# Moving eight LoRA matmuls and their copy ahead of a layer norm's broadcast matmul, in the feed-forward stage of a two-stage transformer layer

## The chip, the cores and the metric

One Trainium2 chip, all 8 of its cores. Each core gets 2 of the 16 sequences (2 x 2048 tokens, width 1024) and the same weights, and runs the same program without exchange with the others. The metric is the device time of one execution in microseconds (us), that of the slowest core.

## The reference

```python
x = x + attn(layernorm(x), ...)      # local window attention, latent attention, gates
x = x + ffn(layernorm(x), ...)

def _qlora_linear(x, q, scale, bias, la, lb):
    w = _dequant(q, scale)                       # 4-bit values, a scale for every 16 inputs
    base = einsum('btd,od->bto', x, w) + bias
    lora = einsum('btr,or->bto', einsum('btd,rd->btr', x, la), lb)   # rank 32
    return base + lora

h = x                                            # ffn
for blk in range(3):
    y = _qlora_linear(h, qweights[2*blk], ...)
    y = _layernorm(y, ln_gamma[blk], ln_beta[blk])
    y = gelu(y)
    y = _qlora_linear(y, qweights[2*blk+1], ...)
    h = y + h
```

## The kernel before

The program is written out instruction by instruction for each engine: PE (TensorE, matmuls), DVE (VectorE), ACT (ScalarE), POOL (GpSimd) and SP (which issues transposing DMAs). Each small function adds a stretch to one engine's list. What stands in a list runs in that order; between engines there are counting semaphores (`te` for PE, `ve`, `ev1` and `ev2` for DVE, `sc` for ACT), and a `wait_ge` holds back all that is written behind it on its engine. There is no scheduler: the order of the calls is the order of the work.

The first stage (up to some 2070 us) is the attention, over 16 tiles of 256 tokens. Then the six 1024 x 1024 weight matrices are dequantized into SBUF. The second stage, from about 2210 us, is the feed-forward part, again over 16 tiles of 256 tokens, in 8 pairs of a tile A and a tile B. A pair goes through the three blocks k = 0, 1, 2. Activations lie feature-major, as 8 chunks of 128 features x 256 tokens. For one tile and one block the pieces are:

- `b_Y1`: the first linear map. PE multiplies h by the LoRA factor (L1233, 8 matmuls into bank C6 of psC, 32 x 256); DVE copies the result to SBUF (L1244); PE computes 8 column groups, each of 8 matmuls L1261 and one L1267 that adds the LoRA part. Groups 0 to 3 go to four regions of psA. Group 4 needs region 0 again, group 5 region 1, and so on, and waits until DVE has evacuated groups 0 and 1 (`ev1`).
- `b_L1e`: DVE evacuates the 8 groups with the bias (L1283, two at a time as PE finishes them) and squares them (L1291).
- `b_L1m`: PE sums values and squares over the features with a vector of ones (L1305, L1311, 8 matmuls each).
- `b_L1b`: five one-row operations on DVE (L1326 to L1338, the last a reciprocal), a square root on ACT (L1346, before which it loads its table), and one matmul L1352 on PE that broadcasts mean and inverse deviation to 128 partitions.
- `b_L2`: DVE adds and multiplies them into the tile, two passes over 128 x 2048 (L1366, L1372).
- `b_Ga`: the gelu on ACT, 8 operations (L1386).
- `b_Y2`: the second linear map, built as the first (L1401, L1412, L1429, L1435), with six regions. `b_E2`: DVE evacuates it and adds h (L1456, for the last block L1464); the last count of `ev2` says that the new h is ready.

The two tiles are interleaved: while one is in its layer norm, the other's Y1 runs. The order in a pair, with the part on which the change bears:

```python
for k in range(3):
    b_L1m(A, k)
    b_L1b(A, k)
    if k > 0:
        b_Y1(Bst, k)
        b_L2(A, k)
        b_L1e(Bst, k)
    else:
        b_L2(A, k)
    b_Ga(A, k); b_Y2(A, k); b_E2(A, k)
    b_L1m(Bst, k)
    b_L1b(Bst, k)
    ...                       # the same with b_Y1(A, k + 1) for k < 2
```

"A round" below is the time from one broadcast matmul L1352 to the next; there are 48, and in 32 of them a Y1 follows the broadcast.

Of the kernel before, what the change touches and what calls it, by code (L numbers as in the profile page):

```python
# [68 lines left out]
def build_program():  # L69
# [30 lines left out]
    with contextlib.ExitStack() as es:  # L100
# [10 lines left out]
        ar_t = sb("arena", [128, AC], BF16)  # L111
# [14 lines left out]
        A = lambda n: ar.alloc("A", n)  # L126
# [112 lines left out]
        def I(sem, inst, k=1):  # L239
            sem.n += k  # L240
            inst.then_inc(sem.h, k)
            return sem.n
# [837 lines left out]
        def bank_wait(t, b):  # L1080
            if b in pbank:
                eng, val = pbank[b]
                t.wait_ge({'ve': ve.h, 'sc': sc.h, 'te': te.h,
                           'ev1': ev1.h, 'ev2': ev2.h}[eng], val)

        def bank_set(b, eng, val):
            pbank[b] = (eng, val)
# [123 lines left out]
        def b_hio(st, sbk):  # L1211
            a, bb = st['ha'], st['hb']
            hin = a if sbk != 1 else bb
            hout = bb if sbk != 1 else a
            return o_hF + hin * NCH * TILE, o_hF + hout * NCH * TILE

        def b_Y1(st, sbk):
            i0 = 2 * sbk
            hin_o, _ = b_hio(st, sbk)
            ti, pp = st['ti'], st['pp']  # L1220
            btr_o = st['btr']

            @block.tensor
            def _(t, i0=i0, hin_o=hin_o, sbk=sbk, ti=ti, pp=pp):
                if sbk == 0:
                    t.wait_ge(dtr[pp].h, h0_done_d[ti])
                    if ti == 0:
                        t.wait_ge(ve.h, deq_done)
                else:
                    t.wait_ge(ev2.h, st['h_ready'])  # L1230
                bank_wait(t, 'C6')
                for c in range(NCH):
                    mm = t.matmul(psC[0:32, 0:TILE],  # L1233
                                  laS[:, i0 * NCH * 32 + c * 32:i0 * NCH * 32 + (c + 1) * 32],
                                  V(hin_o + c * TILE, TILE),
                                  start=(c == 0), stop=(c == NCH - 1))
                I(te, mm)
            st['btr1_te'] = te.n

            @block.vector  # L1240
            def _(v, i0=i0, btr_o=btr_o):
                v.wait_ge(te.h, st['btr1_te'])
                bp = (i0 % 2) * 64
                v.tensor_scalar(ar_t.ap()[bp:bp + 32, btr_o:btr_o + TILE],  # L1244
                                psC[0:32, 0:TILE], 1.0, None, ALU.mult)
                bank_set('C6', 've', I(ve, v.drain()))
            st['btr1_ve'] = ve.n

            te_y1 = {}

            @block.tensor
            def _(t, i0=i0, hin_o=hin_o, btr_o=btr_o):
                ev0 = ev1.n
                for oc in range(NCH):
                    reg = Y1REGS[oc % 4]
                    if oc >= 4:
                        t.wait_ge(ev1.h, ev0 + ((oc - 4) | 1) + 1)
                    else:
                        bank_wait(t, Y1BANKS[oc % 4])
                    for c in range(NCH):  # L1260
                        t.matmul(reg, wTv(i0, c, oc * 128, 128),  # L1261
                                 V(hin_o + c * TILE, TILE),
                                 start=(c == 0), stop=False)
                    if oc == 0:
                        t.wait_ge(ve.h, st['btr1_ve'])
                    bp = (i0 % 2) * 64
                    mm = t.matmul(reg,  # L1267
                                  lbS[bp:bp + 32,
                                      (i0 // 2) * 1024 + oc * 128:(i0 // 2) * 1024 + oc * 128 + 128],
                                  ar_t.ap()[bp:bp + 32, btr_o:btr_o + TILE], start=False, stop=True)  # L1270
                    te_y1[oc] = I(te, mm)
            st['te_y1'] = te_y1

        def b_L1e(st, sbk):
            i0 = 2 * sbk
            te_y1 = st['te_y1']
            y1o, sqo = st['y1F'], st['sqF']

            @block.vector
            def _(v, i0=i0, y1o=y1o):  # L1280
                for oc in range(NCH):
                    v.wait_ge(te.h, te_y1[min(oc | 1, NCH - 1)])
                    v.tensor_scalar(V(y1o + oc * TILE, TILE),  # L1283
                                    Y1REGS[oc % 4],
                                    biasS[:, i0 * 8 + oc:i0 * 8 + oc + 1], None, ALU.add)
                    bank_set(Y1BANKS[oc % 4], 'ev1', I(ev1, v.drain()))  # L1286
            st['y1_evac'] = ev1.n

            @block.vector
            def _(v, y1o=y1o, sqo=sqo):  # L1290
                v.tensor_tensor(V(sqo, NCH * TILE), V(y1o, NCH * TILE),  # L1291
                                V(y1o, NCH * TILE), op=ALU.mult)
                I(ve, v.drain())
            st['sq_ve'] = ve.n
# [19 lines left out]
                I(te, mm)  # L1314
            st['sums_te'] = te.n

        def b_L1b(st, sbk):
            sro, bro = st['srow'], st['brow']
            sb_name, sb_ps, sb_off = st['stb']
            sr = lambda a, bn: ar_t.ap()[0:1, sro + 2 * a:sro + 2 * a + 2 * bn].bitcast(F32)  # L1320
            br = lambda a, bn: ar_t.ap()[0:1, bro + a:bro + a + bn]

            @block.vector
            def _(v, sb_ps=sb_ps, sb_off=sb_off):
                v.wait_ge(te.h, st['sums_te'])
                v.tensor_scalar(br(0, TILE), sb_ps[0:1, sb_off:sb_off + TILE],  # L1326
                                -1.0 / D, None, ALU.mult)
                v.drain()
                v.tensor_tensor(sr(0, TILE), br(0, TILE), br(0, TILE), op=ALU.mult)
                v.drain()  # L1330
                v.scalar_tensor_tensor(sr(TILE, TILE),
                                       sb_ps[0:1, sb_off + 256:sb_off + 256 + TILE],
                                       1.0 / D, sr(0, TILE),
                                       op0=ALU.mult, op1=ALU.subtract)
                v.drain()
                v.tensor_scalar(sr(TILE, TILE), sr(TILE, TILE), EPS, None, ALU.add)
                v.drain()
                v.reciprocal(sr(2 * TILE, TILE), sr(TILE, TILE))  # L1338
                I(ve, v.drain())  # L1339
            st['var_ve'] = ve.n  # L1340

            @block.scalar
            def _(s):
                s.wait_ge(ve.h, st['var_ve'])
                with nc.allow_low_precision(reason="bf16 LN inv for broadcast matmul"):
                    I(sc, s.activation(br(TILE, TILE), sr(2 * TILE, TILE), AF.Sqrt))  # L1346
            st['sig_sc'] = sc.n

            @block.tensor
            def _(t, sb_ps=sb_ps, sb_off=sb_off):  # L1350
                t.wait_ge(sc.h, st['sig_sc'])
                mm = t.matmul(sb_ps[:, sb_off:sb_off + 512], onesR[0:1, :], br(0, 512),  # L1352
                              start=True, stop=True)
                I(te, mm)
            st['bc_te'] = te.n
# [156 lines left out]
        for pair in range(nbt_total // 2):  # L1512
            A = b_state(2 * pair)
            Bst = b_state(2 * pair + 1)
            b_Y1(A, 0)
            b_L1e(A, 0)
            b_Y1(Bst, 0)
            b_L1e(Bst, 0)
            for k in range(3):
                b_L1m(A, k)  # L1520
                b_L1b(A, k)
                if k > 0:
                    b_Y1(Bst, k)
                    b_L2(A, k)
                    b_L1e(Bst, k)
                else:
                    b_L2(A, k)
                b_Ga(A, k)
                b_Y2(A, k)
                b_E2(A, k)  # L1530
                b_L1m(Bst, k)
                b_L1b(Bst, k)
                if k < 2:
                    b_Y1(A, k + 1)
                    b_L2(Bst, k)
                    b_L1e(A, k + 1)
                else:
                    b_L2(Bst, k)
                    b_tail(A)
                b_Ga(Bst, k)  # L1540
                b_Y2(Bst, k)
                b_E2(Bst, k)
            b_tail(Bst)
            for tj in (2 * pair + 2, 2 * pair + 3):
                if tj < nbt_total:
                    emit_x2load(tj)
                    emit_ln2_h0(tj)
# [87 lines left out]
```

## Time and profile before

| | us |
|---|---|
| median of 2 runs | 4145.25 |
| the two runs | 4129.68, 4160.83 |
| the profiled execution: device time | 4170.05 |
| its span, first to last instruction, core 4 (the slowest) | 4168.5 |
| the shortest span of a core (core 1) | 4114.9 |
| PE matmuls busy, share of the span | 2569.3, 62% |
| PE weight loads busy | 1621.0, 39% |
| DVE busy | 1981.8, 48% |
| ACT busy | 1009.4, 24% |
| POOL busy | 77.0, 2% |

The times are those of one profiled execution on its slowest core, so sums are made against its own 4170.05 us and not against the median. Matmuls overlap in the engine and their ends are modelled, so the sum of their durations is not the time that PE needs for them; distances from one start to the next are. "Granted clock" is the share of TensorE's full 2.4 GHz that the chip granted in a stretch. In the chain of work that ended last, PE has 44% of the span, DVE 26%, ACT 10%, and 9% is "issue": short pauses in which an engine waits for nothing that the profile shows.

### The profile page before, as it was taken

The numbers are of one execution on the slowest core, as the hardware profiler recorded it, in microseconds if no ns is written. First come the engines' busy times: TensorE is split into PE (matmuls) and PEld (weight loads), VectorE is DVE, ScalarE is ACT, GpSimd is POOL, SyncE is SP. The second block draws the span as 40 slices with busy tenths as digits, with TensorE's granted clock in tenths as the row PEclk, the third lists the DMA queues.
The fourth block names the chain that finished last, engine by engine and source line by source line (L and its number), as shares of the span: only waits on it lengthen the run. The fifth ranks groups of instructions, "written<-read, shape, count | busy, mean of one in ns | idle before, by whom it ended". The sixth has DMA issues, their size and how long they took to land.

```text
span 4168.5 us, 57513 instructions; the slowest of 8 cores (4114.9 to 4168.5 us)
## 1 busy us (share of the span) xinstructions
PE 2569.3 (62%) x20161; PEld 1621.0 (39%) x20176; DVE 1981.8 (48%) x3863; ACT 1009.4 (24%) x1729; POOL 77.0 (2%) x126
## 2 busy tenths in 40 slices
PE   0566666566667666666435757567576666757666
PEld 0344443344444434444203434344343433434333
DVE  1445544454545444555324544445454444545544
ACT  0122233322223333222372212212121221212121
POOL 1000000000000000000020000000000000000000
PEclk9766766666666556666557867778797888878787
DMA  9021111111111111111331010100102010010201
GB/s 136 13 34 29 29 26 29 29 34 29 29 31 24 29 34 29 29 29 26 45 105 36 1 51 1 41 11 6 46 1 51 1 36 16 6 46 1 51 1 31
DMA packets 259705, 128.18 MB, mean 31 GB/s; under 512 B 229232, under 2 KB 233504, under 8 KB 259424
## 3 DMA queue, kind: packets, MB, share of 16 engines
q1 hardware_dynamic: 228864, 79.72, 9.5%
q0 software_dynamic: 30560, 44.79, 5.8%
q8 instruction: 167, 2.74, 0.3%
q14 instruction: 114, 0.93, 0.1%
HBM read 61.99 MB, written 25.17 MB: 21 GB/s over the span
## 4 chain that ended last, share of the span: by engine, by line
PE 44%; DVE 26%; ACT 10%; issue 9%; DMA 5%; another core or an unknown queue 2%; DVEq 2%; SPq 1%; ACTq 1%; POOL 0%; POOLq 0%
PE psA L1261 7%; PE psB L1429 5%; PE psA L1429 4%; DMA arena<-arena 3%; ACT arena L794 3%; PE psA L772 3%; PE psB L891 3%; PE psA L384 2%; DVE arena L1372 2%; DVE arena L1366 2%; PE psA L413 2%; DVE arena L1338 2%; DVE arena L806 2%; DVE arena L1283 2%
## 5 line engine op out<-in xcount | busy, mean ns | idle before, releaser
L1261 PE MATMUL psA<-arena,wbig 128*128 128x256 bf16 x3072 | 457.4, 299 | 24.6 <-DVEq L1286 24.6
L772 PE MATMUL psA<-arena 64*128 64x256 bf16 x960 | 249.9, 391 | 170.1 <-ACT arena L794 170.1
L1261 PEld LDWEIGHTS psA<-arena,wbig 128*128 128x128 bf16 x3072 | 292.6, 105 | 137.8 <-issue 56.4
L806 DVE TENSOR_TENSOR arena<-arena,mlocS 128x512 bf16<-128x512 bf16 x480 | 204.1, 425 | 228.2 <-ACT arena L794 203.7
L1346 ACT ACT_TABLE_LOAD x48 | 61.6, 1283 | 1008.3 <-DVEq L1339 1008.3
L1283 DVE TENSOR_SCALAR arena<-psA,biasS 128x256 bf16<-128x256 f32 x384 | 185.9, 484 | 237.3 <-PE psA L1267 191.3
L794 ACT ACTIVATE arena<-psA 128x512 bf16<-128x512 f32 x480 | 260.9, 594 | 59.9 <-PE psA L772 58.8
L1429 PE MATMUL psA<-arena,wbig 128*128 128x256 bf16 x1536 | 222.6, 293 | 0.0
L384 PE MATMUL psA<-wbig,arena 128*128 128x512 bf16 x497 | 140.6, 448 | 131.9 <-DMA arena<-arena 121.8
L1429 PE MATMUL psB<-arena,wbig 128*128 128x256 bf16 x1536 | 205.5, 278 | 0.0
L772 PEld LDWEIGHTS psA<-arena 64*128 64x128 bf16 x960 | 72.9, 106 | 319.2 <-issue 310.2
L1386 ACT ACTIVATE arena<-arena,lnbS,lngS 128x256 bf16<-128x256 bf16 x384 | 193.9, 586 | 0.6
L545 ACT ACT_TABLE_LOAD x16 | 20.5, 1283 | 710.1 <-PE psC L475 710.1
L1233 PE MATMUL psC<-arena,laS 128*32 128x256 bf16 x384 | 84.1, 394 | 159.6 <-DMA arena<-arena 98.7
L833 PE MATMUL psB<-arena 128*128 128x64 bf16 x960 | 79.7, 209 | 150.4 <-DVEq L809 134.1
L1401 PE MATMUL psC<-arena,laS 128*32 128x256 bf16 x384 | 63.9, 322 | 167.2 <-ACT arena L1386 167.2
L1429 PEld LDWEIGHTS psA<-arena,wbig 128*128 128x128 bf16 x1536 | 143.5, 104 | 54.2 <-issue 16.2
L1429 PEld LDWEIGHTS psB<-arena,wbig 128*128 128x128 bf16 x1536 | 136.3, 99 | 38.5 <-issue 0.4
L1386 ACT ACT_TABLE_LOAD x48 | 61.6, 1283 | 345.8 <-DVEq L1375 345.8
L459 PE MATMUL psA<-arena,wbig 128*128 128x256 bf16 x1024 | 128.4, 293 | 24.9 <-DVEq L906 22.0
L833 PEld LDWEIGHTS psB<-arena 128*128 128x128 bf16 x960 | 73.3, 121 | 177.4 <-issue 177.4
L891 PE MATMUL psB<-arena,wbig 128*128 128x256 bf16 x1024 | 131.3, 295 | 12.2 <-DMA arena<-arena 9.1
(166 smaller groups left out, 4304.8 us busy)
## 6 DMA issues: line engine op xcount, KB each, us to landing
y<-arena SPq DMA_DIRECT2D x16, 1024.0 KB, 4.3
arena<-qT POOLq DMA_DIRECT2D x48, 256.0 KB, 2.6
arena<-x_in POOLq DMA_DIRECT2D x16, 512.0 KB, 6.9
x2scr<-arena SPq DMA_DIRECT2D x16, 512.0 KB, 3.4
arena<-x2scr POOLq DMA_DIRECT2D x16, 512.0 KB, 6.2
arena<-arena SPq DMA_TRANSPOSE x224, 3.2
wbig<-wq POOLq DMA_DIRECT2D x1, 2048.0 KB, 18.3
wbig<-wk POOLq DMA_DIRECT2D x1, 2048.0 KB, 30.4
```

The costliest lines, as they stand in the source:

```text
L384: mm = t.matmul(reg, V(o_XF + c * TILE + tc * 128, 128), wv_(o_wv + c * 1024 + og * 512, 512), start=(c == 0), stop=(c == NCH - 1))
L459: mm = t.matmul(reg, wv_(o_wk + c * 1024 + oc * 128, 128), V(o_XF + c * TILE, TILE), start=(c == 0), stop=(c == NCH - 1))
L772: mm = t.matmul(reg[:, hh * 256:(hh + 1) * 256], ar_t.ap()[0:64, o_KR + h * 2 * W + sl * W + koff: o_KR + h * 2 * W + sl * W + koff + 128] ...
L794: sc_exp[nb] = I(sc, s.activation(dst, reg, AF.Exp))
L806: v.tensor_tensor(dst.rearrange("p (g q) -> p g q", g=2), dst.rearrange("p (g q) -> p g q", g=2), mkv, op=ALU.mult)
L833: mmA = t.matmul(avreg[:, h * 64:(h + 1) * 64], st, V(o_VR + vsl * 1024 + h * 64, 64), start=first, stop=last)
L891: mm = t.matmul(reg, wv_(o_wo + c * 1024 + oc * 128, 128), V(o_mixF + c * TILE, TILE), start=(c == 0), stop=(c == NCH - 1))
L1233: mm = t.matmul(psC[0:32, 0:TILE], laS[:, i0 * NCH * 32 + c * 32:i0 * NCH * 32 + (c + 1) * 32], V(hin_o + c * TILE, TILE), start=(c == 0), ...
L1261: t.matmul(reg, wTv(i0, c, oc * 128, 128), V(hin_o + c * TILE, TILE), start=(c == 0), stop=False)
L1283: v.tensor_scalar(V(y1o + oc * TILE, TILE), Y1REGS[oc % 4], biasS[:, i0 * 8 + oc:i0 * 8 + oc + 1], None, ALU.add)
L1386: I(sc, s.activation(V(go + c * TILE, TILE), V(go + c * TILE, TILE), AF.Gelu, bias=lnbS[:, sbk * 8 + c:sbk * 8 + c + 1], scale=lngS[:, sbk ...
L1429: t.matmul(reg, wTv(i1, c, oc * 128, 128), V(go + c * TILE, TILE), start=(c == 0), stop=False)
```

## The change

`b_Y1` is split after the copy of the LoRA product (`b_Y1a` up to there, `b_Y1b` the column groups), and `b_L1b` is split before the broadcast matmul (`b_L1v` the row operations and the root, `b_L1c` the broadcast). In the pair's loop the other tile's `b_Y1a` now stands between `b_L1v` and `b_L1c`. At the start of a pair `b_Y1` is still called whole.

```diff
-        def b_Y1(st, sbk):
+        def b_Y1a(st, sbk):
...
             st['btr1_ve'] = ve.n
 
+        def b_Y1b(st, sbk):
+            i0 = 2 * sbk
+            hin_o, _ = b_hio(st, sbk)
+            btr_o = st['btr']
             te_y1 = {}
...
             st['te_y1'] = te_y1
 
+        def b_Y1(st, sbk):
+            b_Y1a(st, sbk)
+            b_Y1b(st, sbk)
+
...
-        def b_L1b(st, sbk):
+        def b_L1v(st, sbk):
...
             st['sig_sc'] = sc.n
+
+        def b_L1c(st, sbk):
+            bro = st['brow']
+            sb_name, sb_ps, sb_off = st['stb']
+            br = lambda a, bn: ar_t.ap()[0:1, bro + a:bro + a + bn]
 
             @block.tensor
...
             for k in range(3):
                 b_L1m(A, k)
-                b_L1b(A, k)
+                b_L1v(A, k)
                 if k > 0:
-                    b_Y1(Bst, k)
+                    b_Y1a(Bst, k)
+                b_L1c(A, k)
+                if k > 0:
+                    b_Y1b(Bst, k)
                     b_L2(A, k)
                     b_L1e(Bst, k)
                 else:
...
                 b_L1m(Bst, k)
-                b_L1b(Bst, k)
+                b_L1v(Bst, k)
                 if k < 2:
-                    b_Y1(A, k + 1)
+                    b_Y1a(A, k + 1)
+                b_L1c(Bst, k)
+                if k < 2:
+                    b_Y1b(A, k + 1)
                     b_L2(Bst, k)
                     b_L1e(A, k + 1)
```

PE's list in the second stage, where a tile B's layer norm (statistics in psD) meets the next block's Y1 of tile A, before the change:

```order
L1305 MATMUL psD<-arena,onesS 1x256 x8
L1311 MATMUL psD<-arena,onesS 1x256 x8
L213 UNCONDITIONAL_BRANCH
L1352 MATMUL psD<-arena,onesR 128x512
L213 UNCONDITIONAL_BRANCH
L1233 MATMUL psC<-arena,laS 32x256 x8
L213 UNCONDITIONAL_BRANCH
L1261 MATMUL psA<-arena,wbig 128x256 x8
L1267 MATMUL psA<-arena,lbS 128x256
```

And the same place after it, where L1313 and L1319 are the sums, L1365 the broadcast, and L1265 and L1271 the column groups:

```order
L1313 MATMUL psD<-arena,onesS 1x256 x8
L1319 MATMUL psD<-arena,onesS 1x256 x8
L213 UNCONDITIONAL_BRANCH
L1233 MATMUL psC<-arena,laS 32x256 x8
L213 UNCONDITIONAL_BRANCH
L1365 MATMUL psD<-arena,onesR 128x512
L213 UNCONDITIONAL_BRANCH
L1265 MATMUL psA<-arena,wbig 128x256 x8
L1271 MATMUL psA<-arena,lbS 128x256
```

The eight LoRA matmuls L1233 have gone from behind the broadcast to ahead of it, and nothing else has changed places. With them goes their wait for the h of their own tile.

DVE's list at the same place, after the change (L1346 is the reciprocal, L1379 and L1385 the two normalizing passes, L1291 the evacuations):

```order
L1346 RECIPROCAL arena<-arena 1x256
L213 UNCONDITIONAL_BRANCH
L1244 TENSOR_SCALAR arena<-psC 32x256
L213 UNCONDITIONAL_BRANCH
L1379 TENSOR_TENSOR arena<-arena,psD 128x2048
L1385 TENSOR_TENSOR arena<-arena,psD 128x2048
L213 UNCONDITIONAL_BRANCH
L1291 TENSOR_SCALAR arena<-psA,biasS 128x256 x8
```

It is the order that DVE had before (with the lines L1338, L1366, L1372 and L1283): the copy L1244 already stood between the reciprocal and the first pass. What moved for DVE is only what the copy waits for, which now comes ahead of the broadcast on PE.

## Rows read from the trace of the kernel before

**Rows 1.** Spans and mean granted clocks of two of the cores

```profile
core 0: 4123.3 us, clock 0.752
core 4: 4168.5 us, clock 0.730
```

**Rows 2.** Waits, second stage: engine, line, waited for: us, times, longest

```profile
DVE arena L1244 <- PE psC L1233: 145.3, 39, 4.7
...
PE psD L1352 <- ACT arena L1346: 144.7, 24, 6.9
```

**Rows 3.** Chain that ended last, through one round: start us, us, what

```profile
3026.26 0.58 PE psA L1352
3026.84 1.83 PE psC L1233 x8
...
3028.77 0.41 DVE arena L1244
...
3029.37 2.29 DVE arena L1366
...
3060.18 0.58 PE psD L1352
```

**Rows 4.** Timeline, same round: start us, us, engine, line [idle before <-releaser]

```profile
3019.56 0.48 DVE L1456 SCALAR_TENSOR_TENSOR arena<-psA,biasS,arena 128x256 bf16<-128x256 f32 x1 [0.19 <-issue]
3019.58 1.04 PE L1311 MATMUL psA<-arena,onesS 128*1 128x256 bf16 x8
...
3022.56 1.74 DVE L1338 RECIPROCAL arena<-arena 1x256 f32<-1x256 f32 x1
...
3026.26 0.58 PE L1352 MATMUL psA<-arena,onesR 1*128 1x512 bf16 x1 [5.64 <-ACT arena L1346]
...
3026.77 1.89 PE L1233 MATMUL psC<-arena,laS 128*32 128x256 bf16 x8
...
3028.59 1.89 PE L1261 MATMUL psA<-arena,wbig 128*128 128x256 bf16 x8
...
3030.73 1.41 PE L1261 MATMUL psA<-arena,wbig 128*128 128x256 bf16 x8
...
3035.43 4.04 ACT L1386 ACTIVATE arena<-arena,lnbS,lngS 128x256 bf16<-128x256 bf16 x8
...
3035.55 1.03 PE L1261 MATMUL psA<-arena,wbig 128*128 128x256 bf16 x8 [0.81 <-DVEq L1286]
...
3040.29 1.05 PE L1401 MATMUL psC<-arena,laS 128*32 128x256 bf16 x8
```

**Rows 5.** A round without Y1, and all psD broadcasts (min/median/max ns)

```profile
2994.83 0.58 PE L1352 MATMUL psD<-arena,onesR 1*128 1x512 bf16 x1 [6.51 <-ACT arena L1346]
...
2995.52 2.29 DVE L1366 TENSOR_TENSOR arena<-arena,psD 128x2048 bf16<-128x2048 bf16 x1 [2.65 <-PE psD L1352]
...
L1352 PE MATMUL psD<-arena,onesR x24: 578/580/581, 2248.5 to 4097.1; 1*128 1x512 bf16 x24
```

**Rows 6.** Busy times by stretch; the number behind POOL is the granted clock

```profile
3020.60:3024.70 4.10, 0.02 (x1) 0.00 (x0) 3.26 (x5) 0.29 (x1) 0.00 (x0) 1.00 0.00 0
3024.70:3031.50 6.80, 5.24 (x22) 2.84 (x23) 2.54 (x2) 1.41 (x2) 0.00 (x0) 0.50 0.00 0
...
2563.90:2567.30 3.40, 3.35 (x14) 1.86 (x15) 0.66 (x2) 0.00 (x0) 0.00 (x0) 0.50 0.00 0
...
3127.30:3133.90 6.60, 6.57 (x27) 3.39 (x27) 3.79 (x3) 0.00 (x0) 0.00 (x0) 0.50 0.01 2
...
2529.50:2564.00 34.50, 26.91 (x178) 16.76 (x178) 17.63 (x26) 7.02 (x11) 0.00 (x0) 0.81 0.01 1
2564.00:2597.50 33.50, 24.79 (x177) 15.91 (x178) 17.63 (x26) 7.02 (x11) 0.00 (x0) 0.91 0.00 0
2782.00:2817.80 35.80, 26.59 (x177) 16.73 (x178) 17.63 (x26) 7.02 (x11) 0.00 (x0) 0.88 0.00 1
2792.60:2796.00 3.40, 3.40 (x16) 2.01 (x16) 0.97 (x2) 2.65 (x6) 0.00 (x0) 0.50 0.02 5
```

## The prediction

> **What bounds the kernel now.** I read the spans of the cores first, then the waits of the second stage (the feed-forward part, from 2245 us on), then the chain that ended last through one round of it, then that round's timeline, and last the granted clock of short stretches.
>
> Core 0 needs 4123.3 us, core 4 as the slowest 4168.5, with the same program and no exchange between them, so the end is the slowest core's own work [rows 1]. In the second stage the broadcast matmul L1352 waits for ACT's square root: 144.7 us in the 24 executions that use psD (the 24 with psA read alike). DVE's copy L1244 waits for PE's L1233: 145.3 us in 39 cases [rows 2]. So the engines hand one chain to and fro, and none is full.
>
> The chain shows where it runs [rows 3]. A round goes from one L1352 to the next, 3026.26 to 3060.18, 33.92 us. Its beginning is: broadcast 0.58; eight LoRA matmuls L1233 1.83; copy 0.41; the normalizing pass L1366, 2.29, and its twin L1372; two evacuations L1283; and only then, at 3035.55 [rows 4], the fifth column group of Y1, since that group wants a bank that DVE has to empty. The 36 matmuls of Y1 that PE already did in between are not on the chain there. The LoRA matmuls have nothing to do with this tile's normalization: they are there because both engines run in written order.
>
> The timeline has the place they could go [rows 4]. PE ends L1311 at 3020.62 and starts L1352 at 3026.26, idle for 5.64 us, while DVE does five one-row operations (the last, L1338, ends at 3024.30) and ACT then loads a table and takes the root, which releases L1352.
>
> **The change part by part.** Per tile pair the split step is used four times (the two k > 0 rounds of tile A and the two k < 2 rounds of tile B), so 4 x 8 pairs = 32 times. In the other 16 rounds no Y1 stands between broadcast and L2, and nothing moves. No instruction is added or dropped.
>
> *LoRA matmuls into the gap.* They cost 1.89 us at the low clock, and at the high one 1.05 us, which L1401's like-sized eight took [rows 4]. Either fits into 5.64 us. They need h, whose last evacuation ends at 3020.04, before L1311 itself ends [rows 4]; so the wait that now stands ahead of the broadcast holds nothing up. Cost nothing, bounds 0 to 0; without that cover the broadcast would be late by 1.89 us less the idle time.
>
> *The copy L1244.* It now stands right behind L1338 with its input ready. From 3024.30 it would end, with the 0.19 us that follow such a hand-over and its own 0.41, at about 3024.9. Queued behind it on DVE is only L1366, which waits for the broadcast (3026.26) anyway. The cover is 1.3 us of root and table load; if it were gone, 0.6 us.
>
> *What the broadcast now releases.* In the rounds without Y1, L1366 starts 0.69 us after L1352 (2994.83 to 2995.52) [rows 5]; in the others 3.11 us after (3026.26 to 3029.37) [rows 3]. All of DVE's work up to the second evacuation therefore comes 2.42 us earlier: the fifth group's bank is free 9.29 - 2.42 = 6.87 us after the broadcast. This is the most that the change can give, 2.42 us a round.
>
> *What is late next.* PE itself. Y1 now starts where L1233 started, 0.51 us after the broadcast (3026.77), not 2.33 (3028.59) [rows 4]. Four groups of nine matmuls must pass before the fifth. One group takes 2.14 us at the 1.2 GHz level (3028.59 to 3030.73) and 1.19 us at the 2.4 GHz level (four from 3035.55 to 3040.29, 4.74) [rows 4]. The broadcast finds PE at the low level each time: 578 to 581 ns in the 24 executions with psD, as in the one with psA shown [rows 4, 5]. Here the clock was granted at 0.50 until 3031.5, 5.2 us after the broadcast [rows 6]. With the clock back X us after the broadcast, the fifth group starts at 0.51 + 4 x 1.19 + (X - 0.51) x (2.14 - 1.19) / 2.14. The lows seen end 3.4 us (2563.9 round) to 6.6 us (3127.3 round) after the broadcast [rows 6]. That gives 6.55, so DVE's 6.87 decides, to 7.97; with 5.2 it is 7.35. Against 9.29 the gain is 2.42, 1.32 and 1.94 us. Until now PE waited 0.81 us there for DVE, which is why these differences in the clock did not show in a round's length. I take 1.9.
>
> *Behind the fifth group* nothing changes: the evacuations there wait for PE, Y1 ends that much earlier, DVE squares and copies, and PE's wait for that copy before Y2's first L1435 stays. The gelu has to be in time for the next LoRA matmuls L1401. It follows L1372, moves by the full 2.42, and was done at 3039.47 against L1401's start at 3040.29 [rows 4]; it remains ahead.
>
> *The sum.* 32 x 1.9 = 61 us, with bounds 32 x 1.32 = 42 and 32 x 2.42 = 77. The profiled execution took 4170.05 us around a span of 4168.5, and lies 24.8 us above the median 4145.25; the gain per round hangs on neither. From the profile's own time 4170 - 61 = 4109; from the median 4145 - 61 = 4084 us, 1.5% less.
>
> What is written of the clock: the Trainium skill (TensorE: Matmul & The Clock Gate, "HAM oscillation") says that waits between bursts of matmuls drop the array to half its clock and each burst then starts cold, and so that filling the gap may keep it warm. The trace agrees on the drop: PE idle from 3020.6, granted 1.00 until 3024.7 and then 0.50 [rows 6]. By that rule taken at its best the round starts warm and the sum is the 77 us of the second case below; by the rows the gap shrinks from 5.64 us to 4.6 only, and I leave the clock as it is.
>
> **The rivals.**
>
> *The clock stays up.* With matmuls in the gap the clock could be 1.00 at the broadcast. For it: the low began only 4.1 us into the idle time here, and 4.6 us is left. Against: no broadcast with psD ran faster than 578 ns [rows 5]. Then four groups end at 0.51 + 4.76 = 5.27, DVE's 6.87 decides, 32 x 2.42 = 77 us: 4068.
>
> *The whole die is slowed more often.* In the 2529.5 round the granted clock averaged 0.81 and the round took 34.50 us; the next one, 0.91 and 33.50, with the same instructions [rows 6]. A PE with fewer pauses could draw this state in nearly all rounds of the slowest core. Then some 27 of 32 rounds lose 0.9 us, 24 us: 61 - 24 = 37, 4108. Against: over the span the two cores shown differ by 0.752 to 0.730 only [rows 1]. The Trainium skill speaks of this against the change (same page, Part 1, the peak-current limiter: a third core of a die in dense matmuls takes the die to 13/16); the level 0.81 agrees. By it alone the time would be this case's.
>
> *It does not do what it says.* Something keeps the broadcast or L1366 where it was, most likely a hand-over of some 2 us in the gap that the rows do not show. Gain 0: 4145. Against: both inputs are ready beforehand, above.
>
> *Slower: the low clock outlasts the gain.* The place is Y1 right after the broadcast, where the moved matmuls no longer stand in the slow stretch, so that Y1's own do. Y1 alone would end at 0.51 + 8 x 1.19 + 0.444 x (X - 0.51), against 14.03 us today (3026.26 to 3040.29); this turns into a loss from X = 9.5 us on. In the longest low here X was 6.6, but in the 2782.0 round a second low of 3.4 us came at 2792.6, within Y1, and that round took 35.80 [rows 6]. If the clock stays low through all of Y1, it ends at 0.51 + 8 x 2.14 = 17.6, 3.6 us later than now: 32 x 3.6 = +115, 4260 us.
>
> **How the numbers follow.** The forecast has 0.63, the clock that stays up 0.16, the slowed die 0.12, no effect 0.05, the slower case 0.04. The forecast's own range is 4068 to 4103. The median of two runs (4129.68 and 4160.83) leaves some 10 us on either side, and the slowed die lies at 4108; with those the range is 4056 to 4112, and what is left out is the last two cases and the tails of the rest. Two per cent, about what a measurement of this kernel can tell from no change, is 83 us: beyond the 77 of the ceiling. Faster by more than that takes the clock that stays up or the ceiling, and a favourable measurement: 0.12. Slower by more than 2% is nearly all of the last case: 0.03. Within 2%: 0.85.
>
> **What would show it.** Right: eight L1233 between L1311 and the broadcast; PE's idle time before the broadcast 4.6 us or less, and its start still 5.6 us after the sums; L1366 0.69 us after the broadcast in all 48 rounds; the wait of L1244 for PE gone outside the first rounds; the fifth group 6.9 to 8.0 us after the broadcast; rounds of 31.1 to 32.3 us in place of 33.5 to 33.9; the first stage untouched. Wrong: broadcasts in 0.4 us (clock up, second case); more rounds at 0.81; rounds that shrink by less than 1.3 us although L1366 is early, which would mean a limit behind Y1 that I did not see; or a fifth group after 9.3 us.

## The result, and the profile after the change

| | before | after |
|---|---|---|
| median, us | 4132.92 (10 runs) | 4073.18 (11 runs) |
| lowest and highest | 4126.98, 4172.93 | 4060.3, 4130.07 |
| profiled execution, span of its slowest core | 4168.5 (core 4) | 4060.1 (core 1) |
| core 0 of the profiled executions | 4123.3 | 4058.1 |
| ratio after to before | | 0.9845, 95% interval 0.9809 to 0.9880 |

The ratio says 1.55% off, which is 64 us of 4132.92; the medians differ by 60. The spans of the two profiled executions differ by 108 us, which is more: core 4 of the one before ran parts of both stages at a granted clock of 0.81 (its mean was 0.730), and the change has no share in that. Core 0 had 0.752 before and 0.747 after, and is the fairer pair: 65.2 us, or 2.04 us for each of the 32 rounds. Pairs of single cores scatter (55 us on core 1, 80 us on core 2). What does not scatter is the sum of the 32 rounds with a Y1, from broadcast to broadcast: on core 0 it fell from 1076.6 to 1012.5 us, by 64.1 us or 2.00 us a round. Before, it was 1076.3 to 1076.6 us on six cores (1084.7 and 1082.5 on cores 4 and 5); after, 1009.7 to 1012.5 on all eight.

Spans and mean granted clocks after, to be set beside [rows 1]:

```profile
core 0: 4058.1 us, clock 0.747
core 1: 4060.1 us, clock 0.750
```

The timeline of one round after (line numbers are those of the changed kernel: L1319 the sums, L1346 the reciprocal, L1365 the broadcast, L1379 the first normalizing pass, L1265 the column groups), to be set beside [rows 4]. PE's rows:

```profile
2280.13 1.04 PE L1319 MATMUL psD<-arena,onesS 128*1 128x256 bf16 x8
2281.23 1.03 PE L1233 MATMUL psC<-arena,laS 128*32 128x256 bf16 x8
2286.81 0.37 PE L1365 MATMUL psD<-arena,onesR 1*128 1x512 bf16 x1 [4.55 <-ACT arena L1354]
2287.11 1.67 PE L1265 MATMUL psA<-arena,wbig 128*128 128x256 bf16 x8
...
2293.47 1.03 PE L1265 MATMUL psA<-arena,wbig 128*128 128x256 bf16 x8
...
2317.76 0.37 PE L1365 MATMUL psA<-arena,onesR 1*128 1x512 bf16 x1 [4.77 <-ACT arena L1354]
```

and DVE's:

```profile
2283.11 1.74 DVE L1346 RECIPROCAL arena<-arena 1x256 f32<-1x256 f32 x1
2285.04 0.41 DVE L1244 TENSOR_SCALAR arena<-psC 32x256 bf16<-32x256 f32 x1 [0.19 <-issue]
2287.29 2.29 DVE L1379 TENSOR_TENSOR arena<-arena,psD 128x2048 bf16<-128x2048 bf16 x1 [1.84 <-PE psD L1365]
...
2292.81 0.48 DVE L1291 TENSOR_SCALAR arena<-psA,biasS 128x256 bf16<-128x256 f32 x1 [0.19 <-issue]
```

The LoRA matmuls stand in the gap and leave 4.55 us of it, the copy follows the reciprocal after 0.19 us, and the first pass starts 0.48 us after the broadcast where it was 3.11 [rows 3]. The fifth group (2293.47) starts 6.66 us after the broadcast in place of 9.29, and the round takes 30.95 us. It is one of the shortest. In a longer one of the same core the broadcast finds the low clock, four groups take until 8.0 us, and the round takes 32.31:

```profile
3048.84 0.58 PE L1365 MATMUL psD<-arena,onesR 1*128 1x512 bf16 x1 [4.78 <-ACT arena L1354]
3049.35 1.89 PE L1265 MATMUL psA<-arena,wbig 128*128 128x256 bf16 x8
...
3056.85 1.05 PE L1265 MATMUL psA<-arena,wbig 128*128 128x256 bf16 x8
...
3081.15 0.58 PE L1365 MATMUL psA<-arena,onesR 1*128 1x512 bf16 x1 [5.65 <-ACT arena L1354]
```

What differs between the two is when the clock was low. Busy times by stretch, the number behind POOL being the granted clock, to be set beside [rows 6]:

```profile
2282.20:2286.80 4.60, 0.06 (x1) 0.02 (x1) 2.85 (x4) 1.70 (x2) 0.00 (x0) 1.00 0.00 0
2287.40:2290.90 3.50, 3.50 (x17) 1.83 (x15) 3.42 (x2) 0.00 (x0) 0.00 (x0) 0.51 0.00 0
...
3048.50:3055.30 6.80, 6.46 (x27) 3.40 (x27) 5.31 (x4) 1.20 (x2) 0.00 (x0) 0.50 0.01 2
```

In the short round the clock was up over the whole idle stretch and at the broadcast, and low for 3.5 us of Y1 only; in the longer one the low stretch takes 6.8 us. The statistics of all broadcasts (min/median/max ns), to be set beside [rows 5], show that both kinds occur and that the slow one stays the rule; on this core 6 of the 48 took under 0.50 us, all of them among the 32 with a Y1:

```profile
L1365 PE MATMUL psD<-arena,onesR x24: 371/577/581, 2224.4 to 3990.6; 1*128 1x512 bf16 x24
...
L1365 PE MATMUL psA<-arena,onesR x24: 371/578/581, 2255.4 to 4023.0; 1*128 1x512 bf16 x24
```

In the short round the chain that ended last has lost its detour over DVE: it runs from the broadcast into PE's own groups, where before it ran over the copy and the passes [rows 3]. PE and DVE are level there: PE alone would have started the fifth group at 2293.45, and it started at 2293.47, when the second evacuation L1291 (2292.81) had freed its bank. So the short round runs at DVE's limit, and the longer one, whose PE needs until 8.0 us, at PE's.

```profile
2286.81 0.37 PE psD L1365
2287.18 1.60 PE psA L1265 x8
...
2289.11 1.82 PE psA L1265 x8
```

And of the waits of the second stage (engine, line, waited for: us, times, longest), the wait of DVE's copy for PE [rows 2] is gone (1.0 us in 3 cases). DVE now waits for the broadcast itself, and PE's wait for the copy at Y2 is untouched (43.6 us, 31 times, before):

```profile
DVE arena L1379 <- PE psD L1365: 53.2, 24, 2.6
...
PE psA L1448 <- DVEq L1427: 46.0, 32, 1.4
```

### The profile page after: what moved, and what is told of

Read it like the earlier page. It is cut to its first block, busy times and chain, and to the rows that moved or that the text cites. A ratio compares the mean times of both kernels' runs of the same rounds, so it can differ in the third digit from the quotient of the medians.

```text
span 4060.1 us, 57528 instructions; the slowest of 8 cores (4052.9 to 4060.1 us)
## 1 busy us (share of the span) xinstructions
PE 2493.8 (61%) x20176; PEld 1590.6 (39%) x20176; DVE 1981.0 (49%) x3863; ACT 1009.6 (25%) x1729; POOL 76.9 (2%) x126
## 4 chain that ended last, share of the span: by engine, by line
PE 45%; DVE 25%; ACT 10%; issue 9%; DMA 5%; another core or an unknown queue 2%; DVEq 2%; SPq 1%; ACTq 1%; POOL 0%; POOLq 0%
PE psA L1265 11%; PE psB L1442 5%; PE psA L1442 4%; DMA arena<-arena 3%; ACT arena L794 3%; PE psA L772 3%; PE psA L1271 2%; DVE arena L1346 2%; PE psA L384 2%; DVE arena L806 2%; PE psA L459 2%; PE psB L891 2%; ACT arena L1399 2%; ACT L1354 2%
## 5 line engine op out<-in xcount | busy, mean ns | idle before, releaser
L1265 PE MATMUL psA<-arena,wbig 128*128 128x256 bf16 x3072 | 467.1, 303 | 0.5 <-DVEq L1294 0.2
L1265 PEld LDWEIGHTS psA<-arena,wbig 128*128 128x128 bf16 x3072 | 295.9, 107 | 116.8 <-issue 32.2
L1291 DVE TENSOR_SCALAR arena<-psA,biasS 128x256 bf16<-128x256 f32 x384 | 185.7, 484 | 240.8 <-PE psA L1271 199.0
L1442 PE MATMUL psB<-arena,wbig 128*128 128x256 bf16 x1536 | 201.1, 274 | 0.0
L1414 PE MATMUL psC<-arena,laS 128*32 128x256 bf16 x384 | 63.4, 320 | 167.2 <-ACT arena L1399 167.2
L1233 PE MATMUL psC<-arena,laS 128*32 128x256 bf16 x384 | 56.5, 296 | 159.0 <-DMA arena<-arena 138.6
L384 PEld LDWEIGHTS psA<-wbig,arena 128*128 128x128 bf16 x512 | 52.9, 108 | 209.2 <-issue 170.1
L891 PE MATMUL psB<-arena,wbig 128*128 128x256 bf16 x1024 | 119.5, 276 | 16.7 <-DMA arena<-arena 9.1
```

Of the source, the lines that this page charges most:

```text
L384: mm = t.matmul(reg, V(o_XF + c * TILE + tc * 128, 128), wv_(o_wv + c * 1024 + og * 512, 512), start=(c == 0), stop=(c == NCH - 1))
L891: mm = t.matmul(reg, wv_(o_wo + c * 1024 + oc * 128, 128), V(o_mixF + c * TILE, TILE), start=(c == 0), stop=(c == NCH - 1))
L1265: t.matmul(reg, wTv(i0, c, oc * 128, 128), V(hin_o + c * TILE, TILE), start=(c == 0), stop=False)
L1291: v.tensor_scalar(V(y1o + oc * TILE, TILE), Y1REGS[oc % 4], biasS[:, i0 * 8 + oc:i0 * 8 + oc + 1], None, ALU.add)
L1442: t.matmul(reg, wTv(i1, c, oc * 128, 128), V(go + c * TILE, TILE), start=(c == 0), stop=False)
```

## The experiments

All ratios are to the kernel before, measured on the same chip and at the same time as the run. The runs used four chips in all (e1 to e4 one, e5 to e8 another, e9 and e10 a third, e11 a fourth), so a difference in us between runs of different groups is rougher than the ratios. Rounds and starts are read on the core that is named.

### e1_fill_only: the gap filled, the chain left as it was

```diff
                 if k > 0:
-                    b_Y1a(Bst, k)
+                    b_fill(Bst, k, 8)      # the 8 LoRA matmuls into psC[:, 256:512]
                 b_L1c(A, k)
                 if k > 0:
-                    b_Y1b(Bst, k)
+                    b_Y1(Bst, k)
```

(and the same in tile B's half, here and in all that follow but e7)

> The order of before is kept (broadcast, then L1233, copy, Y1); in the 32 gaps ahead of the broadcast the same eight LoRA matmuls run once more into an unused half of psC. Theory (the gain is the shortened chain broadcast - L1233 - copy - L1366): the chain is as before, so the fifth column group still starts 9.3 us after the broadcast and the time is that of before within 10 us (some 5 us less where the broadcast now finds the high clock). Rival (the gain is the filled gap, through TensorE's clock): 30 to 64 us less than before.

Measured: 4131.15 us, ratio 1.0000 (0.9974 to 1.0026). Timeline of PE, core 5:

```profile
3010.35 1.04 PE L1290 MATMUL psC<-arena,laS 128*32 128x256 bf16 x8
3016.52 0.58 PE L1378 MATMUL psD<-arena,onesR 1*128 1x512 bf16 x1 [5.13 <-ACT arena L1367]
3017.03 1.89 PE L1233 MATMUL psC<-arena,laS 128*32 128x256 bf16 x8
...
3025.80 1.03 PE L1265 MATMUL psA<-arena,wbig 128*128 128x256 bf16 x8 [0.95 <-DVEq L1307]
```

and of all its broadcasts with psD:

```profile
L1378 PE MATMUL psD<-arena,onesR x24: 467/581/582, 2223.5 to 4056.4; 1*128 1x512 bf16 x24
```

The fifth group starts 9.28 us after the broadcast, as before. Eight matmuls in the gap are worth nothing while the copy and the passes stay on the path; the gain of the change is what left the path behind the broadcast. These eight also did not bring the clock back at the broadcast (none took 0.37 us), so this run says nothing of a filling that does; e5 does.

### e2_copy_late: the matmuls moved, the copy behind the passes

```diff
-                    b_Y1b(Bst, k)
                     b_L2(A, k)
+                    b_Y1c(Bst, k)          # DVE's copy L1244, taken out of b_Y1a
+                    b_Y1b(Bst, k)
```

> The changed kernel, but DVE's copy L1244 stands behind the two normalizing passes. Theory: L1366 stays 0.69 us behind the broadcast, the passes end at 5.35, the copy at 5.95, so group 0 of Y1 is finished at 6.4 and three groups of 1.19 us more put the fifth at 9.9 us in place of 7.2: 32 x 2.7 = 85 us more than the changed kernel, about 4158, 0.6% slower than before. Rival (only the place of the matmuls on PE matters, the copy is free wherever it stands): the time of the changed kernel, 4073.

Measured: 4239.43 us, ratio 1.0278 (1.0237 to 1.0320). The sign was right and the size far off: 166 us more than the changed kernel, not 85. PE's timeline, core 7:

```profile
3015.64 0.58 PE L1370 MATMUL psA<-arena,onesR 1*128 1x512 bf16 x1 [4.78 <-ACT arena L1359]
...
3021.75 0.37 PE L1275 MATMUL psA<-arena,lbS 32*128 32x256 bf16 x1 [3.72 <-DVEq L1250]
...
3028.35 1.05 PE L1269 MATMUL psA<-arena,wbig 128*128 128x256 bf16 x8
```

and the granted clock of two stretches:

```profile
3015.60:3028.00 12.40, 8.64 (x36) 4.51 (x36) 5.96 (x5) 5.32 (x9) 0.00 (x0) 0.50 0.00 1
3028.00:3050.00 22.00, 18.44 (x143) 12.31 (x141) 10.62 (x21) 0.00 (x0) 0.00 (x0) 1.00 0.00 0
```

The copy released L1275 at 6.11 us after the broadcast, close to the 5.95 counted. But with a pause of 3.72 us in it the low clock lasted until 12.4 us after the broadcast, the next three groups took 2.1 us each, and the fifth started at 12.7 (12.23 in the mean of the 32 rounds of this core).

### e9_copy_late_fill: is that rest the clock's?

On top of e2's order:

```diff
+                    if oc == 0 and fill:
+                        for c in range(20):
+                            t.matmul(f_ps[0:32, f_off:f_off + TILE], laS[:, ...], wbig.ap()[:, ...], ...)
                     if oc == 0:
                         t.wait_ge(ve.h, st['btr1_ve'])
```

> e2_copy_late took 81 us more than was expected of it: in its trace PE pauses 3.7 us for the late copy, the granted clock stays at 0.50 until some 12 us after the broadcast, and three groups of Y1 take 2.14 us each. Here 20 useless matmuls (32 columns out, 256 in) stand in that pause. Theory (the missing time was the clock's): the clock is back before the groups, the fifth starts at 9.9 to 10.2 us in place of 12.2, 32 x 2.1 = 67 us less than e2_copy_late, about 4170, ratio to before 1.010. Rival (the copy behind the passes costs more on DVE or PE than counted): 4240 as e2_copy_late, or more where the useless matmuls delay Y1.

Measured: 4154.26 us, ratio 1.0068 (1.0045 to 1.0091). PE's timeline, core 7:

```profile
2995.60 0.58 PE L1377 MATMUL psA<-arena,onesR 1*128 1x512 bf16 x1 [4.77 <-ACT arena L1366]
...
2997.93 3.82 PE L1275 MATMUL psD<-wbig,laS 128*32 128x256 bf16 x20
...
3005.48 1.05 PE L1270 MATMUL psA<-arena,wbig 128*128 128x256 bf16 x8
```

The fifth group starts 9.88 us after the broadcast, where e2 had been expected, and 85 us go: the miss of e2 was the clock's. What is left, 4154 against 4073, is the price of a late copy alone: 81 us by the medians and 92 by the ratios, or 2.6 us a round by the starts of the fifth group (9.88 against a mean of 7.28 on core 0 of the changed kernel). So the copy's place in the gap is as much a part of the gain as that of the matmuls.

### e3_pass_twice: DVE's floor put back

```diff
                 mv = ...
+                if twice:                  # in the 32 rounds
+                    v.tensor_tensor(V(go, ...), V(y1o, ...), mv, op=ALU.add)
+                    v.drain()
                 v.tensor_tensor(V(y1o, ...), V(y1o, ...), mv, op=ALU.add)
```

> The changed kernel, but in the 32 rounds DVE runs the first normalizing pass once more into the buffer that the second pass overwrites (+2.37 us on DVE behind the broadcast). Y1 still starts 0.3 to 0.5 us after the broadcast. Theory (DVE's passes set the floor): the fifth group starts at 6.87 + 2.37 = 9.24 us, as before the change, so 32 x 2.0 = 64 us more than the changed kernel, about 4137, no faster than before. Rival (what pays is PE's earlier start of Y1): at most 10 us more than the changed kernel.

Measured: 4147.01 us (4131.40 to 4175.69), ratio 1.0036 (1.0007 to 1.0065). PE's timeline, core 0:

```profile
3012.78 0.58 PE L1365 MATMUL psD<-arena,onesR 1*128 1x512 bf16 x1 [4.78 <-ACT arena L1354]
3013.29 1.89 PE L1265 MATMUL psA<-arena,wbig 128*128 128x256 bf16 x8
...
3022.02 1.86 PE L1265 MATMUL psA<-arena,wbig 128*128 128x256 bf16 x8 [1.49 <-DVEq L1294]
```

Y1 starts 0.51 us after the broadcast as in the changed kernel, and the fifth group at 9.24 as forecast (the mean of the 32 rounds too). The whole gain is gone. PE's early start is worth nothing where DVE's passes are 2.37 us later: below PE there is a floor, and it is DVE's. The median is 10 us above the expected 4137; core 0 took 4129.5 us, against 4123.3 before.

### e7_half_the_rounds: tile A's rounds alone

```diff
                 b_L1m(Bst, k)
                 b_L1v(Bst, k)
-                if k < 2:
-                    b_Y1a(A, k + 1)
                 b_L1c(Bst, k)
                 if k < 2:
-                    b_Y1b(A, k + 1)
+                    b_Y1(A, k + 1)
```

> The change in the 16 rounds that begin with tile A's broadcast alone; those of tile B have the order of before. Theory (a gain of 2.0 us per round, round by round): 16 x 2.0 = 32 us less than before, about 4101. Rival (the gain needs the two tiles in step, or is one of the whole stage): 0 or the full 60 us.

Measured: 4104.99 us, ratio 0.9927 (0.9900 to 0.9954). Half the rounds, half the gain: core 0 took 4090.5 us, 32.8 less than before's 4123.3. Its 32 rounds with a Y1 add up to 1045.5 us against 1076.6, which is 1.94 us for each of the 16 changed ones; the other 16 kept their 9.29 us to the fifth group.

### e5_fill_more: PE's share of the limit

```diff
                 if k > 0:
                     b_Y1a(Bst, k)
+                    b_fill(Bst, 24)        # 24 useless matmuls, into the other tile's statistics bank
                 b_L1c(A, k)
```

> The changed kernel, with 24 more matmuls of no use (32 columns out, 256 in, 3.2 us at the high clock) behind the moved LoRA matmuls in the 32 gaps. Theory (DVE's floor and TensorE's clock together set the fifth group): the clock stays up, every broadcast is fast, the fifth group always starts at the floor of 6.66 us and the rounds take 30.95 in place of 31.6 us on average: 32 x 0.65 = 21 us less than the changed kernel, about 4052. Rival (the clock cannot be held this way, or a denser PE draws the granted clock of 0.81): no gain, 4073 or more.

Measured: 4067.91 us (4038.06 to 4126.73), ratio 0.9822 (0.9628 to 1.0016): unclear. The profiled execution (4096.87 us) says why. PE's timeline, core 0:

```profile
3012.10 0.37 PE L1376 MATMUL psA<-arena,onesR 1*128 1x512 bf16 x1 [2.16 <-ACT arena L1365]
...
3013.95 1.89 PE L1265 MATMUL psA<-arena,wbig 128*128 128x256 bf16 x8
...
3018.76 1.03 PE L1265 MATMUL psA<-arena,wbig 128*128 128x256 bf16 x8
```

All 32 broadcasts of core 0 were fast and all fifth groups started 6.66 us after them: the first part of the theory holds. The clock did not stay up, though. The second group takes 1.89 us as at the low level, and the granted clock of the stretch from the broadcast to the fifth group is

```profile
3012.10:3018.80 6.70, 6.65 (x38) 3.74 (x39) 5.54 (x4) 1.45 (x2) 0.00 (x0) 0.75 0.00 0
```

so about half of it, 3.4 us, was low, as in the short round of the changed kernel. By the prediction's formula four groups then end at 0.30 + 4.76 + 0.444 x 3.4 = 6.6 us, just inside DVE's 6.66. The filling made the low stretch shorter and moved it behind the broadcast; it did not abolish it.

But the cores of one die had another clock:

```profile
core 0: 4039.1 us, clock 0.761
...
core 5: 4095.3 us, clock 0.736
```

Core 0 gains 19 us on its 4058.1 in the changed kernel, as the 21 expected; core 5 gives it back, and the slowest core is the time. In two of the four executions no die had that clock, and they took 4038.06 and 4038.96 us, 21 to 22 us less than the shortest of the changed kernel. So the theory of the fifth group holds, and the median hides it. Whether the added matmuls drew the lower clock is not settled. The kernel before, measured at the same time, had a die with a lowered clock in 7 of its 13 executions and took up to 4244.10 us, so they are not needed for it. And in the profiled execution only cores 4 and 5 had it among their added matmuls (0.75 and 0.74 from 3200 to 4000 us, 0.86 on the six others); cores 6 and 7 had it in their first stage, where nothing was added (0.67 up to 2000 us, against 0.70 and 0.71).

### e4_squares_later and e10_squares_alone: the next wait on the chain

```diff
                     b_L2(A, k)
-                    b_L1e(Bst, k)
+                    b_L1e(Bst, k, False)   # evacuations without the squares
                 b_Ga(A, k)
-                b_Y2(A, k)
+                b_Y2(A, k, Bst if k > 0 else None)   # LoRA matmuls and copy, the other tile's squares, groups
```

> The changed kernel, and in the 32 rounds the squares of the other tile (1.23 us on DVE) stand behind the copy of Y2's LoRA product and not ahead of it. Theory (behind Y1 the chain runs last evacuations - squares - copy - first L1448): PE's wait of 1.44 us before Y2's first group shrinks to 0.2 us, 32 x 1.24 = 40 us less than the changed kernel, about 4033, 2.4% faster than before. Rival (the wait only moves, to Y2's evacuations or the sums): no gain over 4073.

> The kernel before with the second step alone: the squares behind the copy of Y2's LoRA product. Theory (it shortens another part of the same chain): PE's wait of 1.44 us at Y2 shrinks to 0.2 us in 32 rounds, 40 us less than before, ratio 0.990, and the fifth group stays at 9.29 us, so that no phase of the clock gives part of it back (with the change it gained 33). Rival (it needs the change's early Y1): no gain.

Measured: e4, with the change, 4040.54 us, ratio 0.9791 (0.9763 to 0.9818), 33 us less than the changed kernel. e10, on the kernel before, 4095.90 us, ratio 0.9908 (0.9894 to 0.9923), 37 us less than before. DVE and PE in e4, core 3:

```profile
3021.35 0.42 DVE L1430 TENSOR_SCALAR arena<-psC 32x256 bf16<-32x256 f32 x1 [0.19 <-issue]
3021.88 1.23 DVE L1304 TENSOR_TENSOR arena<-arena 128x2048 bf16<-128x2048 bf16 x1
```

```profile
3007.44 0.58 PE L1370 MATMUL psA<-arena,onesR 1*128 1x512 bf16 x1 [4.77 <-ACT arena L1359]
...
3015.06 1.05 PE L1265 MATMUL psA<-arena,wbig 128*128 128x256 bf16 x8
...
3021.93 0.26 PE L1456 MATMUL psA<-arena,lbS 32*128 32x256 bf16 x1
```

The wait at L1456 is gone. Both steps shorten the same chain at two places and add up, but for a few us: in e4 the fifth group of this round starts 7.62 us after its broadcast (7.53 in the mean, against 7.28 on core 0 of the changed kernel), and no broadcast of this core was fast, where the changed kernel had some. In e10 PE waits for DVE at the fifth group anyway (9.29 us), so nothing was there to be given back.

### e6_squares_fill, e8_squares_fill_all and e11_fill_longer: both, with useless matmuls against the low clock

```diff
                 if k > 0:
                     b_Y1a(Bst, k)
+                    b_fill(Bst, 24)        # e6
+                else:
+                    b_fill(Bst, 32)        # e8, e11: the rounds without Y1 too
                 b_L1c(A, k)
...
                     b_L2(A, k)
+                    b_fill(Bst, 56)        # e8, e11: while PE waits for the gelu
...
                     b_L2(Bst, k)
+                    b_fill(A, 56)          # e8; 80 in e11
```

> e4_squares_later with the same 24 matmuls in the 32 gaps. There the fifth group started 7.54 us after the broadcast and no broadcast was fast. Theory: with the clock up it starts at 6.66, 32 x 0.88 = 28 us less than e4_squares_later, about 4012. Rival as in e5_fill_more: 4040 or more.

> e6_squares_fill, with 32 useless matmuls in the gap of the other 16 rounds and 56 behind their broadcast, where PE waits 10.4 us for the gelu and then starts Y2 at the low clock. Theory: L1414 and two groups of Y2 run at the high clock, (1.89 - 1.05) + 2 x 0.95 = 2.7 us, and the broadcast's 0.2 us, so 16 x 2.9 = 46 us less than e6_squares_fill, about 3966. Rival (the denser PE draws the clock of 0.81 on a die): the rounds gain less than 1 us on the slowest core, 4000 or more.

> e8_squares_fill_all gained 19 us of the 46 expected. In its trace the rounds that open a pair lost the expected 2.4 us, but in those that close one (tile B, k = 2) the broadcast found the high clock, the 56 useless matmuls were over after 6.3 us, PE idled 4.2 us and Y2 started at the low clock all the same. Here these rounds get 80 of them (9.0 us). Theory (the clock falls in the idle time that is left): 1.5 us of idle time remain, Y2 starts at the high clock, 8 x 2.7 = 21 us less than e8_squares_fill_all, about 3967. Rival (something else bounds the closing rounds): 3988.

Measured: e6 4006.73 us, ratio 0.9701 (0.9677 to 0.9724), 34 us under e4 where 28 were expected. e8 3987.87 us, ratio 0.9657 (0.9624 to 0.9691), 19 us under e6 where 46 were expected. The 19 are the opening rounds': 31.40 us in the mean in e6 and 29.08 in e8 (core 0), eight times. PE's timeline of e8, core 0, first the eight LoRA matmuls of an opening round, then a round that closes a pair:

```profile
2231.31 1.03 PE L1430 MATMUL psC<-arena,laS 128*32 128x256 bf16 x8 [1.58 <-ACT arena L1415]
...
2367.75 0.37 PE L1381 MATMUL psA<-arena,onesR 1*128 1x512 bf16 x1 [2.15 <-ACT arena L1370]
2368.05 6.29 PE L1288 MATMUL psD<-wbig,laS 128*32 128x256 bf16 x56
2378.57 1.87 PE L1430 MATMUL psC<-arena,laS 128*32 128x256 bf16 x8 [4.24 <-ACT arena L1415]
```

The fill was sized for the low clock, ran at the high one, and left 4.24 us in which the clock fell again. e11's longer fill did there what was expected: the closing rounds of core 0 are 2.8 us shorter, and in one that was looked at 1.71 us of idle time were left and L1430's eight took 1.03 us. But now the broadcast of six of its eight opening rounds found the high clock, and there the unchanged 56 were over too early: these rounds took 30.4 to 31.1 us in place of 29.1. The profiled execution went from 3986 to 3977 us where 3967 was expected. The six times spread from 3977 to 4062, median 4014.49, ratio 0.9713 (0.9653 to 0.9774), with one die's granted clock lower in the long ones; whether the longer fill drew it is as open as in e5. So e8 is the best version that is shown: 2.1% under the changed kernel and 3.4% under the one before.

## Why the prediction was right

The forecast was 4084 us, 61 less than before; measured were 60 less, at 4073 us (64 by the ratio), since the kernel before came out at 4132.92 in more runs and not at 4145.25. By its steps:

- *Nothing is lost in the gap.* Shown. PE's idle time ahead of the broadcast, mostly 5.65 us before (5.64 to 6.28), is mostly 4.78 us after (4.55 to 5.41 on the 32 rounds), 0.87 us less; the sign "4.6 us or less" was a little too strict, since the eight matmuls take the gap 0.87 us and not 1.05. The copy ended 1.36 us before the broadcast (2285.45 to 2286.81), as estimated. e2 and e9 show what is lost where the copy has no such cover: some 80 to 90 us.
- *DVE's passes come 2.42 us earlier, and that is the floor.* Shown by the timeline and by e3, which puts 2.37 us back and has the fifth group at 9.24.
- *PE is late next, by the clock.* Shown. Between the broadcast at 2954.54 and its fifth group the same core had the clock at 0.50 for 5.3 us and the group started at 7.4; the formula gives 0.51 + 4.76 + 0.444 x 4.8 = 7.4. The groups started 6.66 to 8.1 us after the broadcast where 6.87 to 7.97 was said. The forecast of 7.35 came from the low stretch of a single round, and that this round lay near the mean (7.28 on core 0) was partly luck. e5, with the low stretch cut to about 3.4 us, has them all at 6.66.
- *1.9 us a round.* Measured 2.00 on core 0, from broadcast to broadcast, and 1.94 in e7's half of the rounds.
- *The ceiling of 2.42* was 0.2 too low: I had taken the broadcast at its slow 0.58 us. Where it finds the high clock it takes 0.37, the first pass starts after 0.48 and the fifth group's bank is free at 6.66. The short round shown, 30.95 us, is 2.6 under the 33.5 of [rows 6]. This half of the rival "the clock stays up" came true in some rounds only (6 of the 32 on core 1, 4 on core 0), and in all 32 only with e5's fill. Its other half, that the clock then stays up through the four groups, did not: in the short round shown the clock was low for 3.5 us of Y1, and in e5's for about 3.4. That cost nothing, since PE's 6.6 us lie just inside DVE's floor.
- *Nothing changes behind the fifth group.* Shown: the wait at L1448 is 46.0 us in all, 32 times 1.4, and e4 and e10 took it away, with the change and without it.
- *The slowed die* did not decide the median, but it was no idle rival: it lengthened single runs of the changed kernel and made e5 unclear. Its price was set too low. The 0.9 us came from a round that had this clock in a part only (0.81 from 2534 to 2548 us; that the mean of the whole round is 0.81 too is chance, since some 7 us at 0.50 are in it); on core 5 of e5 a round spent in it took 33.97 us (3241.65 to 3275.62) against 30.95, which is 3 us. In e5's profile the four cores of one die had means of 0.736 to 0.746 and those of the other 0.759 to 0.761. The Trainium skill (TensorE: Matmul & The Clock Gate, Part 1) has the whole die at 13/16 once three of its cores are in dense matmuls. The traces agree with a state of the die at that level (0.81 in the stretch just named), but the other die ran the same program without it, so this rule alone does not say when it comes. That more matmuls bring it on is not settled by these runs.
- *The slower case*, a low clock that outlasts the gain, did not come in the change, whose lows ended 6.9 us after the broadcast at the latest (core 1). It came in e2, where the copy was late as well: a low clock until 12.4 us after the broadcast, beyond the 9.5 from which a loss was expected, and 2.8% more than before.

## What to carry to other kernels

Where engines run in written order, look on the chain for work that belongs to something else, and see whether its inputs are ready before the wait ahead of it; move the whole of it, here the copy on the other engine as well, since half a move was worth less than none (e2). Filling a gap gains nothing while another engine sets the pace (e1), and gains something where PE's clock does (e6): count what leaves the path, then what the next engine allows, and test that limit by putting the same time back (e3). And price a new pause of PE at the clock, not only at its length: with 3.7 us of waiting the matmuls behind it took so much longer that 85 us went in 32 rounds, 2.7 us each (e2 against e9).

## What was not expected of the hardware

- The low clock is not a fixed toll. After nearly the same idle time it ended 3.5 to 6.9 us after the broadcast where PE went on working (core 1 of the changed kernel), and 12.4 us after it in the round of e2 that is shown, where PE paused for 3.72 us in between. With useless matmuls in that pause (e9) the groups behind it ran at the high clock.
- Matmuls whose result nobody reads count for the clock. In e5, 24 of them left 2.16 us of idle time before the broadcast, and all 32 broadcasts of core 0 ran at the high clock (0.37 us). A low stretch remained behind it, of about 3.4 us in the round shown in place of 6.8 in the long round of the changed kernel. e6, with them, is 34 us faster than e4 without.
- With a gap of 4.24 us left over in e8 the clock fell (L1430's eight matmuls took 1.87 us, against 1.03 where the gap was 1.58 us in the opening rounds of the same core).
